# Sorting a graph's edges: bucket flags built with buckets innermost, and lookups that read PSUM

## The reference

```python
support = x @ W;  r_D = sigmoid(support @ a2);  gated = r_D * support
msg = gated[col] * edge_values[:, None]
out = segment_sum(msg, row, num_segments=n)
sumnorm = segment_sum(edge_values * r_D[col, 0], row, num_segments=n)
out = out / sumnorm[:, None]            # then two nonlinear steps
x = x + graph_layer(layernorm(x), [src, dst], edge_weight, ...)
x = x + slice_attention(layernorm(x), ...)
```

## Time and profile before

| | |
|---|---|
| median of three runs | 1522.57 us |
| profiled execution, own time | 1522.95 us |
| its span, first to last instruction | 1521.1 us |
| PE busy | 1260.8 us (83%) |
| DVE busy | 1021.0 us (67%) |
| POOL busy | 998.7 us (66%) |
| ACT busy | 357.6 us (24%) |

### The profile page before, as it was taken

The page is one execution under the profiler, slowest core; times in us unless marked ns, Lnnn a source line. Parts: engine busy times, 40 slices in busy tenths (PEclk is TensorE's granted clock), DMA queues, the critical chain, the costliest instruction groups (busy, mean ns, idle before and its releaser), DMA issues.

```text
span 1521.1 us, 21470 instructions
## 1 busy us (share of the span) xinstructions
PE 1260.8 (83%) x6147; PEld 900.7 (59%) x6147; DVE 1021.0 (67%) x2790; ACT 357.6 (24%) x1174; POOL 998.7 (66%) x969
## 2 busy tenths in 40 slices
PE   4888788788888887767888888888888888888998
PEld 3666577667776666534555454645545555455787
DVE  7865998879777686344866766667676677765322
ACT  0433111111000000001332333333233333323232
POOL 0567477777777777767777777777777777771000
PEclk9899788989998899878999999999999999989999
DMA  8111344465444444556444445444444444441022
GB/s 257 51 55 52 37 111 121 116 135 140 125 133 129 133 130 132 139 111 116 115 116 111 115 115 114 117 113 114 116 109 115 112 115 115 111 111 52 22 76 72
DMA packets 158694, 166.47 MB, mean 109 GB/s; under 512 B 84303, under 2 KB 129251, under 8 KB 158588
## 3 DMA queue, kind: packets, MB, share of 16 engines
q0 software_dynamic: 42848, 114.59, 28.7%
q1 hardware_dynamic: 94572, 31.24, 8.9%
q10 hardware_dynamic: 21168, 19.35, 4.2%
HBM read 136.73 MB, written 28.38 MB: 109 GB/s over the span
## 4 chain that ended last, share of the span: by engine, by line
POOL 32%; PE 24%; issue 19%; DMA 11%; DVE 11%; POOLq 2%; ACT 1%; SPq 0%; DVEq 0%; ACTq 0%
PE bank L1617 23%; POOL rows L796 19%; POOL rows L699 11%; DMA rows<-gated_rows_dram,ring_i 7%; DVE big L889 2%; POOLq L788 2%; DVE big L920 1%; POOL sorted_edges_dram L687 1%; DMA rows<-gated_rows_dram,lg 1%; DVE big L1006 1%; DMA sorted_edges_dram<-big,idx 1%; DMA srec<-sorted_edges_dram 1%; DVE big L881 1%; DVE S L1068 1%; DVE big L897 0%
## 5 line engine op out<-in xcount | busy, mean ns | idle before, releaser
L1617 PE MATMUL bank<-rows,S 128*128 128x257 f32 (+1 forms) x2254 | 655.2, 415 | 156.1 <-DMA rows<-gated_rows_dram,ring_i 111.9
L796 POOL DMA_INDIRECT rows<-gated_rows_dram,ring_i x564 | 545.3, 967 | 177.6 <-issue 157.6
L1617 PEld LDWEIGHTS bank<-rows,S 128*128 128x128 f32 x2254 | 415.3, 201 | 359.5 <-DMA rows<-gated_rows_dram,ring_i 205.7
L699 POOL DMA_INDIRECT rows<-gated_rows_dram,lg x294 | 323.4, 1100 | 97.1 <-issue 78.0
L1617 PE MATMUL bank<-big 128*98 128x80 f32 (+2 forms) x1741 | 191.4, 275 | 63.7 <-DVE big L920 62.4
L1617 PEld LDWEIGHTS bank<-big 128*98 128x98 f32 (+1 forms) x1741 | 187.3, 192 | 76.4 <-issue 73.9
L1239 DVE TENSOR_SCALAR S<-iota,lof,srec 128x128 f32<-128x128 f32 x637 | 176.9, 353 | 3.4 <-PE bank L1617 3.3
L1250 DVE TENSOR_TENSOR ag<-bank,ovr 128x257 f32<-128x257 f32 x49 | 20.9, 427 | 200.2 <-PE bank L1617 200.2
L1617 PE MATMUL bank<-big,lg 128*128 128x128 bf16 (+3 forms) x586 | 107.7, 341 | 23.1 <-DVE big L876 14.7
L1617 PE MATMUL bank<-Wxs,xT 128*128 128x512 f32 x196 | 110.8, 693 | 0.1
L1476 ACT COPY ovr<-bank 128x257 f32<-128x257 f32 x98 | 36.6, 374 | 315.6 <-PE bank L1617 309.8
(11 more groups left out here) (243 smaller groups left out, 1412.6 us busy)
## 6 DMA issues: line engine op xcount, KB each, us to landing
overflow_sums_dram<-ovr ACTq DMA_DIRECT2D x98, 128.5 KB
rows<-gated_rows_dram,ring_i POOLq DMA_INDIRECT x564, 2.8
gated_rows_dram<-rows SPq DMA_DIRECT2D x49, 128.5 KB, 2.4
ovr<-overflow_sums_dram SPq DMA_DIRECT2D x49, 128.5 KB, 2.3
out_dram<-S SPq DMA_DIRECT2D x48, 128.0 KB, 1.7
rows<-gated_rows_dram,lg POOLq DMA_INDIRECT x294, 3.0
res<-in_x_dram SPq DMA_DIRECT2D x1, 4352.0 KB
xn<-overflow_sums_dram ACTq DMA_DIRECT2D x33, 128.5 KB, 3.0
```

The lines of the kernel that those rows point to most:

```text
L699: pool.indirect_dma_start(rows[:, turn(n), :], None, gtab[:, :], bass.IndirectOffsetOnAxis(ap=ring1[:, n:n + 1], axis=0)).then_inc(s_row[t ...
L796: pool.indirect_dma_start(rows[:, slot(b, u), :], None, gtab[:, :], bass.IndirectOffsetOnAxis(ap=ring_i[:, b // CH % 2, n:n + 1], axis=0)) ...
L1617: return nc.tensor.matmul(o, l, r, start=start, stop=stop, skip_group_check=True)
```

## The change

1. `flag(g)` now builds the flags with buckets innermost, in two buffers (`flagsj[k]`), and folds those. The flags with columns innermost (`flags4`, one buffer) come from a new step `mark(g)`. `spread_flags` is gone, and so is the table `buckets`.
2. The bucket numbers that `flag` and `mark` compare with are `iota2` in PSUM from group 8 on, and `iotab` in SBUF up to group 7 (`numbers`).
3. `lookup(g)` reads the lane sums from `bank[0]` in PSUM, not from `base2`. So `above(g+1)` waits for `lookup(g)` (`s_prod`), no longer for ACT's copy (`s_bs`), and the copy no longer waits for an older lookup.
4. `above(g)` takes its column `j` from the new layout, where the 49 buckets of one column lie side by side.
5. `mark(g+1)` stands at the end of DVE's loop `g`; for the groups 0 and 1 it stands before `lookup(0)` and after `later(1)`.

```diff
-        flags4 = [halved(carve(NB * HC, BF16), HC) for k in range(2)]
-        flagsj = carve(NB * HC, BF16).rearrange("p (n b) -> p n b", b=NB)
-        folded = [halved(carve(NB * HC // 2, BF16), HC // 2) for k in range(2)]
+        flags4 = halved(carve(NB * HC, BF16), HC)
+        flagsj = [carve(NB * HC, BF16).rearrange("p (h j b) -> p h j b", h=2, b=NB) for k in range(2)]
+        folded = [carve(NB * HC // 2, BF16).rearrange("p (h j b) -> p h j b", h=2, b=NB) for k in range(2)]
...
-            v.tensor_copy(buckets.rearrange("p b h j -> p b (h j)"), iotab[:, 0:NB].unsqueeze(2).broadcast_to([P, NB, GC]))
...
+            def numbers(g):
+                return iota2 if g > G1 + 2 else iotab[:, 0:NB]
+
             def flag(g):
                 k = g % 2
                 if g >= 2:
                     dve.wait_ge(s_base, g - 1)
-                step(v.tensor_tensor(flags4[k],
-                                     hib[:, g * GC:(g + 1) * GC].rearrange("p (h j) -> p h j", h=2).unsqueeze(1)
+                step(v.tensor_tensor(flagsj[k], hib[:, g * GC:(g + 1) * GC].rearrange("p (h j) -> p h j", h=2).unsqueeze(3)
+                                     .broadcast_to([P, 2, HC, NB]),
+                                     numbers(g).unsqueeze(1).unsqueeze(1).broadcast_to([P, 2, HC, NB]), ALU.is_equal))
+                v.tensor_tensor(folded[k], flagsj[k][:, :, 0:HC // 2, :], flagsj[k][:, :, HC // 2:HC, :],
+                                ALU.add).then_inc(s_flag, 1)
+
+            def mark(g):
+                step(v.tensor_tensor(flags4, hib[:, g * GC:(g + 1) * GC].rearrange("p (h j) -> p h j", h=2).unsqueeze(1)
                                      .broadcast_to([P, NB, 2, HC]),
-                                     buckets, ALU.is_equal))
-                v.tensor_tensor(folded[k], flags4[k][:, :, :, 0:HC // 2], flags4[k][:, :, :, HC // 2:HC],
-                                ALU.add).then_inc(s_flag, 1)
-
-            def spread_flags(g):
-                b = iota2 if g > G1 + 1 else iotab[:, 0:NB]
-                step(v.tensor_tensor(flagsj, hib[:, g * GC:(g + 1) * GC].unsqueeze(2).broadcast_to([P, GC, NB]),
-                                     b.unsqueeze(1).broadcast_to([P, GC, NB]), ALU.is_equal))
+                                     numbers(g).unsqueeze(2).unsqueeze(3).broadcast_to([P, NB, 2, HC]), ALU.is_equal))
...
             def lookup(g):
-                k = g % 2
                 dve.wait_ge(s_bs, g + 1)
-                v.tensor_tensor(halved(prod[:, 0:NB * GC], HC), flags4[k],
-                                base2[k][:, :, 0, :].rearrange("p h b -> p b h").unsqueeze(3).broadcast_to([P, NB, 2, HC]),
+                v.tensor_tensor(halved(prod[:, 0:NB * GC], HC), flags4,
+                                bank[0][:, 0:4 * NB].rearrange("p (h v b) -> p h v b", h=2, v=2)[:, :, 0, :].rearrange("p h b -> p b h").unsqueeze(3).broadcast_to([P, NB, 2, HC]),
                                 ALU.mult).then_inc(s_prod, 1)
...
                 hot(g, 1)
+                if g + 1 < NG:
+                    mark(g + 1)
...
-                    act.wait_ge(s_prod, g - 1)
...
                 if g:
-                    pe.wait_ge(s_bs, g)
+                    pe.wait_ge(s_prod, g)
                 for j in range(HC // 2):
-                    m = mm(bank[0][:, 0:4 * NB], lowerb, folded[k][:, :, :, j].rearrange("p b h -> p h b").unsqueeze(2).broadcast_to([P, 2, 2, NB]), j == 0, j == HC // 2 - 1)
+                    m = mm(bank[0][:, 0:4 * NB], lowerb, folded[k][:, :, j, :].unsqueeze(2).broadcast_to([P, 2, 2, NB]), j == 0, j == HC // 2 - 1)
```

More of the change, by code:

```diff
@@ L198, in build @@
         rank2 = bank[4][:, 2 * GC:3 * GC]
-        buckets = halved(carve(NB * HC, BF16), HC)
         prod = carve((NB + HC) * HC, BF16)
@@ L889, in values @@
                     m = v.tensor_tensor(hot_v[h][:, :, i, :],
-                                        flagsj[:, h * HC:(h + 1) * HC, :],
+                                        flagsj[g % 2][:, h, :, :],
                                         w.unsqueeze(2).broadcast_to([P, HC, NB]), ALU.mult)
@@ L963, in _ @@
             later(0)
+            mark(0)
             lookup(0)
             centre()
-            spread_flags(0)
             for h in range(2):
@@ L970, in _ @@
             later(1)
+            mark(1)
             for h in range(2):
@@ L1088, in _ @@
                     step(v.tensor_copy(vals2, packew.rearrange("p (v n) -> p v n", v=2)[:, :, g * GC:(g + 1) * GC]))
-                spread_flags(g)
                 values(g, 0)
```

## The result

The changed kernel takes 1485.99 us in the median of 4 runs (1484.69 to 1489.32), the kernel before, measured beside it, 1522.40: ratio 0.977, 95% interval 0.975 to 0.979. The forecast was 1489.0, range 1480 to 1507.

The account below looks back on a forecast made before the run. POOL was taken to set the time from the first gather on, its gathers held by DVE. Loops 7 to 25 -32.6, before the first gather -1.4, loop 6 0: -34.0 us from 1522.95, forecast 1489, range 1480 to 1507.

Parts of the forecast that it names:

- POOL's hold in loops 7 to 25: Sort loops 7 to 25: gathers held by DVE's two-SBUF-input passes cost 38.7 us; 6.1 would remain, gain 32.6 us.
- The estimate by chance starts: Loops 7 to 25: gathers starting at random on fold (0.13 us) or line 897 (0.19) cost 6.1 us in 19 loops.
- rival C: Sort loops: the hold moves to the next operations, POOL gains under 6 us; 1516 to 1522 us, chance 0.05.
- The pair: Loops 7 to 25: nearly all of POOL's 38.7 us are gathers held at lookup and flag, one in each loop.
- DVE: Loops 7 to 13 and 14 to 25: DVE needs 17.5 and 18.1 us per loop, just below POOL's 18.4 and 22.1.
- B: Partial gain: DVE falls behind in loops 7 to 13, fold stays in step, or PE slows; 1497 to 1512 us, chance 0.22.
- cover: DVE's slack: place's waits for sends, 5.1 us each; in loops 7 to 13 less than 1 us per loop stays.
- The place waits: Place on DVE waited for sends 87.3 us in 17 waits; forecast under 50 us in total.
- Above: Eight matmuls on PE: contiguous operand cuts 2.98 us to 0.84, taken as 2.1 us less per above.
- Before the first gather: Start and groups 1 to 6: 4.1 + 1.8 + 0.8 + 2.6 - 10.7 = -1.4 us, bounds -4 and +7.
- Loop 6: POOL's loop 6: lookup and spread stop holding, flag(7) and mark(7) hold longer; 0 us, bounds -3 and +2.
- The sum: Whole kernel: -32.6 - 1.4 + 0 = -34.0 us from the profiled 1522.95.

Follow-up runs that it names:

- experiment 1: Changed kernel with lookup reading its lane sums from SBUF again: 1716.76 us, ratio 0.993 on a slower chip; repeated on a usual-clock chip, 1511.01 us, ratio 0.992.
- experiment 4: Kernel before with only lookup's sums read from PSUM: 1724.26 us, ratio 0.997 on a slower chip; repeated at the usual clock, 1498.11 us, ratio 0.980.
- experiment 6: Changed kernel with two further VectorE passes, PSUM to PSUM, at the head of each group 7 to 25: 1489.95 us, ratio 0.977.
- Experiment 7: Changed kernel with above's eight matmuls run three times over: 1494.81 us, ratio 0.980.
- experiment 5: The changed kernel itself, nothing altered, run again on a second chip: 1489.47 us, ratio 0.977 to the kernel before.
- experiment 8: Changed kernel with later's bucket numbers and loop 6's values, ranks and bucket numbers also read from PSUM: 1486.90 us, ratio 0.974.
- experiment 9: Kernel of experiment 8 with the second set of gather indices computed early, right after quad: 1479.18 us, ratio 0.971.
- experiment 10: Changed kernel with only the second set of gather indices computed early, right after quad: 1486.60 us, ratio 0.975.
- the second of 1: Repeat, on a chip with the usual clock, of the changed kernel with lookup's sums from SBUF: 1511.01 us, ratio 0.992.
- experiment 3: Changed kernel with folded flags written in the old layout, so above reads at a 32-byte stride and fold writes strided: 1759.43 us, ratio 1.017, slower chip.
- experiment 2: Changed kernel with flag's and mark's bucket numbers read from SBUF in every group: 1716.60 us, ratio 0.994, slower chip.

## Why the prediction was right

*POOL's hold in loops 7 to 25.* Forecast -32.6, measured -34.3; loops of 391.6 us against 393.3. Of the miss of 1.7 us, 1.0 is a count: the earlier trace rows lists 207 instructions in loops 14 to 25, but 206 DMAs start there (182 gathers and 24 sends), so POOL was over its undisturbed time by 39.7 us and not 38.7. What was left is 5.0 us, forecast 6.1; only 3.5 of it lie at the two operations of the forecast, fold 0.4 and not 2.5, later 3.1 and not 3.6. The estimate by chance starts took every start inside an operation as held. But a held gather ends 0.83 us after the holder and an undisturbed one 0.953 us after its start, so by these two numbers a start in the holder's last 0.12 us isn't lengthened; with that the same estimate gives 1.5 for fold and 2.5 for later, 4.0 in all. The experiments show the cause: held time and length of the loops move together, by 21 and 21 us in experiment 1 and by 27.6 and 27.6 in experiment 4. No gather of loops 8 to 25 is over 1.5 us, the mean of the 294 gathers of line 698 is 0.99 us (forecast near 0.97, before 1.10), and rival C, a hold that moves on, did not come.

*The pair.* I priced lookup and flag as one hold without telling them apart. Experiments 1 and 4 do: lookup in PSUM alone brings 27.6 us, and the rest of the change about 7 in these loops.

*DVE.* Forecast 17.5 and 18.1 us busy per loop; 17.3 and 18.0 came. Passes with a PSUM operand cost nothing measurable: 1779 ns against 1781 for lookup. The gain was not cut by DVE, so B fell, but my worry rested on a wrong reading of cover (experiment 6): what counts is how long DVE's own loop is against POOL's and how far it is ahead, not whether it waits. The place waits became 41.0 us in 13 (forecast under 50).

*Above.* Forecast 0.84 us, came 0.85 wherever PE ran at full clock. At half clock it is 1.47 to 1.49, which I left out: above(2) and (6) in after, at 70.66 and 171.24, with a granted clock of 0.50. Above(0) and (1) took 1.46 and 1.47 too, though the profile lists a granted clock of 1.00 there; why is open. Before it was 2.98 to 2.99 at 1.00 and at 0.50 (above(2) at 65.88). Experiment 7 shows it on the path before the first gather and off it behind.

*Before the first gather.* Forecast -1.4, the profile showed +0.5, within bounds of -4 and +7. The statistics begin 4.0 us later (42.16, before 38.15); the forecast's terms up to there make 3.8 (4.1 for the later above(1), 1.8 for mark(1), less 2.1 for a shorter above(1)). What this execution lost against the forecast is above(1) and (2), which cost 0.6 each more than counted, and the clock: a put of group 2 took 4.25 us at a granted 0.67 where before's took 2.97 at 1.00. That makes 2.5 together. Against that stands how much this moment varies: in six further executions with the same start and the same above (experiments 5, 6, 8, 9, 10 and the second of 1) it lies at 178.7 to 181.1, 180.0 on the average, where 180.3 was forecast. Since before was profiled in one execution only, neither the 0.5 nor the forecast's -1.4 can be told from such a scatter.

*Loop 6.* Forecast 0, came +0.2. I weighed holds gone against holds longer, and they did balance (POOL busy 19.60 us before, 19.79 after). But this was not what fixed the loop: with all its holds gone it still took 23.6 us, because DVE made the next indices as late as the holds had ended (experiments 8 to 10). A forecast that took the holds alone off loop 6 would have failed.

*The sum* was -34.0 and the profiled executions differ by 33.6. That this is nearer than its two larger terms is luck: 1.7 us too little at POOL's hold and 1.9 too much before the first gather cancel. The medians differ by 36.4, within the spread of both.

## What to carry to other kernels

When another engine's queue stretches at certain moments, look for the operation beside it and ask where its operands lie, not only how long it takes: a slower pass with one operand in PSUM was the better one here. Work that follows a wait may be bound twice by limits of equal length; if removing the first changes nothing, look at what the engine now waits for before giving it up. And an engine without any wait is not yet the bound: count the other engine's own steps, and see which sum gives the loop.

## What the runs showed of the hardware

- A bf16 addition of 784 elements took 0.593 us when it wrote contiguously and 3.509 us when it wrote every 32 bytes, with inputs contiguous both times (experiment 3). Matmuls of 196 columns reading every 32 bytes took 2.98 us for eight at a granted clock of 1.00 and 2.99 at 0.50, contiguous ones 0.85 and 1.47.
- A held gather ended 0.83 us after the pass that held it: lookup, a lookup in after's order (512.40 and 511.57), a flag (467.16 and 466.33). The strided fold of experiment 3 is an exception (fold 467.81 to 471.27, gather 468.88 to 471.64, 0.37 us after it), which stays open.
- Two holders that overlap hold as one: in the earlier trace rows flag starts 0.08 us before lookup ends, and the gather waits for both. Fold, which starts 0.04 us after the flag's end, did not prolong it, there and in experiment 2.
- On a chip that granted TensorE 0.82 to 0.85 instead of 0.92 the kernel before took 13% longer (1730 against 1525 us), and its time hid the cause: in the kernels of experiments 1, 2 and 4, which differ by 22 us in held time, POOL waited 63 to 91 us in loops 7 to 25 and the medians lie within 8 us. Held time, summed over the DMAs, told the same there as on the faster chip (20.0 and 21.05 us at lookup, 10.3 and 12.1 in before with lookup in PSUM).
